# Both key halves of the probability-value products in one unit of TensorE's order

## The chip, the cores and the metric

The kernel runs on one core of a Trainium2 chip (trn2). The metric is the device time of one execution in microseconds. TensorE (PE) does the matrix products, ScalarE (ACT), VectorE (DVE) and GpSimd (POOL) the rest; SyncE (SP) issues the DMAs. Each engine works through its own instruction list in order, and they wait for each other on semaphores.

## The reference

The input is 32 batches of 256 tokens with 256 features. Four layers follow one another, each adding to x: an autocorrelation mix of a context, a mixture of 8 experts (router, top 1), an attention with 16 heads over 256 keys, and a gated feed-forward with quantised weights and activations. The part that matters here is the attention:

```
scores = jnp.einsum('bhqd,bhkd->bhqk', q, k) / jnp.sqrt(D_K)
scores = jnp.where(m == 0, NEG, scores)
p_attn = softmax(scores, axis=-1)
x = jnp.einsum('bhqk,bhkd->bhqd', p_attn, v)
```

## The kernel before

After a first stage over all batches (the context mix, up to about 160 us), the batches run through a software pipeline. One step of it starts one new batch and carries each older batch a stage on; some six batches are in work at once. A step is 128 ticks long. The table AT gives each job the tick at which it stands, counted from the batch's start, LATER shifts it on one engine, and CHUNKS says in how many pieces a job comes and how many ticks lie between them. The function pipeline sorts the pieces by tick within the step, for each engine by itself. A tick is only an order: the hardware knows the instruction list and the semaphores, nothing of ticks. The first eight steps and the rest are written out one after another.

The attention of a batch, for 16 heads and two halves of the keys (128 each):

- "max": PE multiplies queries and keys (L1312) into one of two banks, and DVE reduces to the maximum of each row (L1046). The negated maximum is written into an extra row of the query stack.
- "exp": for s = 0 to 15, PE computes the scores, keys on the partitions, of two heads and one key half (L1259) into cbank, which is one bank of PSUM. ACT takes the exponential (L796) into pt[s % 4], a ring of four buffers. Scores s wait for exponential s-1, since there is only one cbank. In s, bit 0 is the pair of heads, bit 1 the key half, and s // 4 the group of four heads.
- "pv": unit u = 0 to 7 (L1274) handles group u // 2 and key half u % 2. It is four matmuls with 32 columns of values each, into the four partition quarters of obank, which reads pt buffers 2u % 4 and 2u % 4 + 1. A matmul of fp32 data shows as two records in the profile, so a unit is eight records. Key half 0 starts the sum and key half 1 ends it. After each unit a semaphore pv_done[u % 2] is raised.
- "out": ACT copies obank to ot (L802), once per group.

The exponential s may overwrite its buffer once the unit that read it is done. With u = s // 2 - 2 it waits for pv_done of unit u, for s = 0 to 3 of the previous batch (units 6 and 7). On PE, unit u stands at tick 499 + 16u, group g's second unit thus at 515 + 32g; on ACT exponential s stands at 486 + 8s and "out" g at 524 + 32g.

On PE, what stands around the units within one step, in order (numbers are pieces; the jobs belong to batches of different age):

```
... v, score 0, xT_a, q, unit 7, route, score 1, h_T 1, norm 0, score 2, norm 1, unit 0,
routeT, down 1, score 3, norm_T, k, gateT, o, gbias, score 4, expert 0, unit 1, max 0,
score 5, max 1, expert 1, max 2, score 6, max 3, expert 2, unit 2, max 4, quant_T, score 7,
... score 8, max 7, gate_up 1, expert 4, unit 3, max 8, score 9, ... expert 6, unit 4, max 12,
... gate_up 5, unit 5, score 13, gate_up 6, h_T 0, max_T, score 14, gate_up 7, unit 6, down 0 ...
```

On ACT, the list reads at the places of interest: h_quant 1, exp 0, xah (xT_a, L747), q (L781), out 3, exp 1; gbias, exp 4, k (L770), out 0, exp 5; gate_up 0, exp 8, expert 3, gate_up 1, out 1, exp 9; h_quant 0, exp 12, expert 7, gate_up 5, out 2, exp 13, hqt (h_T 0, L853), max_T, gate_up 6, exp 14. Other engines' lists hold no pv job.

Of the kernel before, what the change touches and what calls it, by code (L numbers as in the profile page):

```python
# [15 lines left out]
NB, S, D = 32, 256, 256  # L16
# [32 lines left out]
    "load": 0, "x2": 211, "ln_a": 190, "xn_a": 228, "xT_a": 237, "route": 232, "routeT": 226, "gate": 233,  # L49
    "gateT": 257, "gbias": 267, "expert": 266, "k": 266, "k_split": 324, "k_write": 336, "ln_b": 311,  # L50
    "xn_b": 336, "xT_b": 350, "k_read": 440, "q": 363, "q_split": 380, "v": 354, "q_write": 366,
    "q_read": 449, "max": 393, "max_T": 449, "max_row": 619, "exp": 480, "pv": 499, "out": 511, "norm": 619,
    "norm_T": 645, "o": 666, "ln_c": 650, "absmax": 649, "quant": 646, "quant_T": 658, "gate_up": 672,
    "h_max": 710, "h_quant": 703, "h_T": 711, "down": 727, "store": 675,
}
# [24 lines left out]
    },  # L80
}

CHUNKS = {"expert": (8, 8), "max": (16, 4), "exp": (16, 8), "pv": (8, 16), "out": (4, 32), "norm": (2, 8),
          "gate_up": (8, 8), "h_max": (2, 32), "h_quant": (2, 32), "h_T": (2, 32), "down": (2, 32)}

BANKS = {
# [49 lines left out]
def after(eng, sem, b):  # L136

    if b.exists:
        eng.wait_ge(sem, b.n + 1)


def after4(eng, sem, b, k):

    if b.exists:
        eng.wait_ge(sem, b.fours(k))
# [19 lines left out]
def pipeline(eng, name, work):  # L165
# [3 lines left out]
    for order, (job, at) in enumerate(AT.items()):  # L169
        n, apart_by = CHUNKS.get(job, (1, 0))  # L170
        for c in range(n):
# [14 lines left out]
def build(nc, x, ctxT, mask, wq0, bq0, wout_r, bout, rwT, rb, ewT, eb, wqT, bq, wkT, bk, wvT, bv,  # L186
          woT, bo, wgT, wuT, wdT, out):
    with ExitStack() as ctx:
        def sb(name, shape, dt=F32):
            return ctx.enter_context(nc.sbuf_tensor(name, shape, dt))  # L190

        def sem(name):
            return ctx.enter_context(nc.semaphore(name))

        def sems(name, n):
            return [sem(f"{name}{i}") for i in range(n)]
# [67 lines left out]
        va = sb("va", [P, 2, T, H * 32])  # L264
        pt = sb("pt", [P, 4, 2, S])
# [86 lines left out]
        ebank, cbank, obank, maxb = bank[0:2], bank[3], bank[4], bank[7]  # L352
# [47 lines left out]
        sc_ready, ex_made, pv_done, ot_made = sems("sc_ready", 4), sems("ex_made", 4), sems("pv_done", 2), sem("ot_made")  # L400
# [722 lines left out]
        def _(pe):  # L1123
# [41 lines left out]
            for t in range(T):  # L1165
                for g in range(NG):
                    ins = pe.matmul(bank[t][:, 0:S], k0t[:, g, t * P:(t + 1) * P], q0t[:, g], start=(g == 0), stop=(g == NG - 1))
            ins.then_inc(lagstep, 1)

            for t, v in enumerate((bank[4], maxb)):  # L1170
                for g in range(NG):
                    ins = pe.transpose(v[:, g * P:(g + 1) * P], k0t[:, g, t * P:(t + 1) * P], ident[:])
# [5 lines left out]
            for t in range(T):  # L1178
                ins = pe.matmul(bank[2][0:1, 0:S], ones[:, 0:1], lagged[:, t], start=(t == 0), stop=(t == T - 1))
# [3 lines left out]
            for t in range(T):  # L1183
                for k in range(T):
                    ins = pe.matmul(bank[t][:, 0:D], circ[:, k, t * P:(t + 1) * P], wout_s[:, k], start=(k == 0), stop=(k == T - 1))
# [3 lines left out]
            for g in range(NG):  # L1189
                for k in range(T):  # L1190
                    ins = pe.matmul(bank[g // 2][:, (g % 2) * D:(g % 2) * D + D], v0[:, k, g * P:(g + 1) * P], wmix[:, k],
                                    start=(k == 0), stop=(k == T - 1))
# [22 lines left out]
            def work(job, c, b):  # L1215
                shared = shared_bank(job, c)
                par = b.par
                if job == "norm":
# [4 lines left out]
                    for g in range(4):  # L1223
                        ins = pe.transpose(shared[:, g * P:(g + 1) * P], ot[:, g, t * P:(t + 1) * P], ident[:])
                    ins.then_inc(otT_ready[t], 1)
                if job == "norm_T":
                    after(pe, on_made[1], b)
                    use(job, c, b, otn_made)
                    for k in range(KT):
                        for t in range(T):  # L1230
                            ins = pe.transpose(shared[:, k * S + t * P:k * S + (t + 1) * P], on[:, t, k * P:(k + 1) * P], ident[:])
                    ins.then_inc(onT_ready, 1)
                if job == "o":
                    after(pe, otn_made, b)
                    use(job, c, b, o_out)
                    for t in range(T):
                        for k in range(KT):
                            ins = pe.matmul(shared[:, t * D:(t + 1) * D], otn[:, k, t * P:(t + 1) * P], wo[:, k], start=(k == 0), stop=(k == KT - 1))  # L1238
                    ins.then_inc(op_ready, 1)
                if job == "quant_T":  # L1240
# [3 lines left out]
                    for k in range(KT):  # L1244
                        for t in range(T):
                            ins = pe.transpose(v[:, k * S + t * P:k * S + (t + 1) * P], xq[:, t, k * P:(k + 1) * P], identb[:])
                    ins.then_inc(xqT_ready, 1)
                if job == "exp":

                    s = c  # L1250
                    u, key = s // 2, (s // 2) % 2
# [5 lines left out]
                    for j in range(2):  # L1257
                        h = 4 * (u // 2) + 2 * (s % 2) + j
                        ins = pe.matmul(cbank[:, j * S:(j + 1) * S], ks[par][0:AROWS, h, key * P:(key + 1) * P],  # L1259
                                        qs[par][0:AROWS, h, :], start=True, stop=True)  # L1260
                    ins.then_inc(sc_ready[s % 4], 1)
                if job == "pv":

                    u = c
                    g, key = u // 2, u % 2
                    for i in (2 * u, 2 * u + 1):
                        after4(pe, ex_made[i % 4], b, i // 4 + 1)
                    if u == 0:
                        after(pe, va_made, b)
                        after4(pe, ot_made, b.ago(1), 4)  # L1270
                    elif key == 0:
                        after4(pe, ot_made, b, g)
                    for i in range(4):
                        ins = pe.matmul(obank[32 * i:32 * i + 32, 0:S],  # L1274
                                        va[:, par, key, (4 * g + i) * 32:(4 * g + i) * 32 + 32],
                                        pt[:, (2 * u + i // 2) % 4, i % 2], start=(key == 0), stop=(key == 1))
                    ins.then_inc(pv_done[u % 2], 1)
                if job == "gate_up":
                    t, n = c // 4, c % 4
                    if c == 0:  # L1280
# [2 lines left out]
                    for i, w in enumerate((wg, wu)):  # L1283
                        for k in range(KT):
                            ins = pe.matmul(shared[:, i * 256:(i + 1) * 256], xqt[:, k, t * P:(t + 1) * P],  # L1285
                                            w[:, k, n * 256:(n + 1) * 256], start=(k == 0), stop=(k == KT - 1))
                    ins.then_inc(gu_ready[c % 2], 1)
                if job == "h_T":
# [4 lines left out]
                    for k in range(IC):  # L1293
                        ins = pe.transpose(v[:, k * P:(k + 1) * P], hq[:, k * P:(k + 1) * P], identb[:])  # L1294
                    ins.then_inc(hqT_ready[t], 1)
                if job == "down":
# [3 lines left out]
                    for k in range(IC):  # L1300
                        ins = pe.matmul(shared[:, 0:D], hqt[:, k], wd[:, k], start=(k == 0), stop=(k == IC - 1))  # L1301
                    ins.then_inc(dn_ready[t], 1)
                if job == "max":
# [6 lines left out]
                    for j in range(2):  # L1310
                        h = 2 * p + j
                        ins = pe.matmul(shared[:, j * S:(j + 1) * S], qs[par][0:QROWS, h, t * P:(t + 1) * P],  # L1312
                                        ks[par][0:QROWS, h, :], start=True, stop=True)
                    ins.then_inc(mx_ready[t], 1)
                if job == "max_T":
# [3 lines left out]
                    for t in range(T):  # L1319
                        ins = pe.transpose(shared[0:H, t * P:(t + 1) * P], mx[:, t, :], ident[:])  # L1320
                    ins.then_inc(mxT_ready, 1)
                if job == "xT_b":
                    after(pe, xnb_made, b)
                    use(job, c, b, xbt_made)
                    for k in range(KT):
                        for t in range(T):
                            ins = pe.transpose(shared[:, k * S + t * P:k * S + (t + 1) * P], xn[:, t, k * P:(k + 1) * P], ident[:])
                    ins.then_inc(xnb_T, 1)
                if job == "q":
                    after(pe, xbt_made, b)  # L1330
                    use(job, c, b, qh_made)
                    for m in range(KT):
                        for k in range(KT):
                            ins = pe.matmul(shared[:, m * S:(m + 1) * S], wq[:, k, m * P:(m + 1) * P], xbt[:, k], start=(k == 0), stop=(k == KT - 1))
                    ins.then_inc(qp_ready, 1)
                if job == "v":
                    use(job, c, b, va_made)
                    for t in range(T):
                        for k in range(KT):
                            ins = pe.matmul(shared[:, t * D:(t + 1) * D], ct[:, par, k, t * P:(t + 1) * P], wv[:, k], start=(k == 0), stop=(k == KT - 1))  # L1340
                    ins.then_inc(vp_ready, 1)
                if job == "xT_a":
                    after(pe, xna_made, b)
                    use(job, c, b, xal_made)
                    for k in range(KT):
                        for t in range(T):
                            ins = pe.transpose(shared[:, k * S + t * P:k * S + (t + 1) * P], xn[:, t, k * P:(k + 1) * P], ident[:])
                    ins.then_inc(xna_T, 1)
                if job == "route":
# [3 lines left out]
                    for i, (w, v, k) in enumerate(ops):  # L1353
                        ins = pe.matmul(shared[:, 0:S], w[:, k], v[:, k], start=(i == 0), stop=(i == len(ops) - 1))
                    ins.then_inc(rt_ready, 1)
                if job == "routeT":
# [3 lines left out]
                    for t in range(T):  # L1360
                        ins = pe.transpose(shared[:, t * NE:(t + 1) * NE], lt[:, t * P:(t + 1) * P], ident[0:NE, 0:NE])
                    ins.then_inc(rtt_ready, 1)
                if job == "gateT":
                    after4(pe, rchain2, b, 4)
                    use(job, c, b, gt_made)
                    for t in range(T):
                        ins = pe.transpose(shared[0:NE, t * P:(t + 1) * P], gg[:, t], ident[:])
                    ins.then_inc(gT_ready, 1)
                if job == "gbias":
                    after(pe, gt_made, b)  # L1370
                    use(job, c, b, gb_out)
                    for t in range(T):
                        ins = pe.matmul(shared[:, t * D:(t + 1) * D], gt[:, t * P:(t + 1) * P], eb_s[:], start=True, stop=True)  # L1373
                    ins.then_inc(gb_ready, 1)
                if job == "k":
                    landed(pe, c_ld, b, 16)
                    use(job, c, b, kf_made)
                    for m in range(KT):
                        for k in range(KT):
                            ins = pe.matmul(shared[:, m * S:(m + 1) * S], wk[:, k, m * P:(m + 1) * P], ct[:, par, k], start=(k == 0), stop=(k == KT - 1))  # L1380
                    ins.then_inc(kp_ready, 1)
                if job == "expert":
# [7 lines left out]
                    for i, (v, w, k) in enumerate(ops):  # L1390
                        ins = pe.matmul(ebank[t][:, :], v[:, k, t * P:(t + 1) * P], w[:, k, p * 512:(p + 1) * 512],  # L1391
                                        start=(i == 0), stop=(i == len(ops) - 1))
                    ins.then_inc(e_ready[t], 1)

            pipeline(pe, "pe", work)


# [41 lines left out]
```

## Time and profile before

| | |
|---|---|
| median of 3 runs | 1781.84 us (1781.82 to 1786.88) |
| the profiled execution's own time | 1780.0 us |
| its span, first to last instruction | 1778.2 us |
| PE busy | 1570.2 us (88%) |
| DVE, ACT, POOL busy | 1198.3, 1097.4, 771.5 us |
| mean granted PE clock | 0.956 of full |
| chain that ended last, by engine | PE 51%, issue 16%, DVE 16%, POOL 6%, ACT 5%, DMA 5% |

The busy time of an engine is the sum over its instructions with overlaps taken once. The chain is followed back from the last instruction: at each step to what released it, or to the instruction before it on its engine.

### The profile page before, as it was taken

The page shows a single profiled execution, that of the slowest core. Times are in us where ns is not written, and L with a number is a line of the kernel's source. Part 1 is how long each engine was busy: PE and PEld are TensorE (multiplying, and loading weights), DVE is VectorE, ACT ScalarE, POOL GpSimd, SP SyncE. Part 2 cuts the span into 40 slices and gives each one's busy share as a digit, 9 for nine tenths or more (in the row PEclk, how much of TensorE's full clock was granted, in tenths as well). Part 3 has the DMA queues.
Part 4 walks back from the last instruction along what each step waited for, and adds up shares of the span by engine and source line. Part 5 has one row for each costly group of instructions (what it writes and reads, how often), then busy time and mean ns, then how long its engine had stood idle before and what let it go on. Part 6 is the DMA issues. An engine that isn't in the chain of part 4 may idle for free.

```text
span 1778.2 us, 33096 instructions
## 1 busy us (share of the span) xinstructions
PE 1570.2 (88%) x10422; PEld 1160.1 (65%) x10422; DVE 1198.3 (67%) x3300; ACT 1097.4 (62%) x2422; POOL 771.5 (43%) x962
## 2 busy tenths in 40 slices
PE   5935789999999999999999999999999999999764
PEld 4824556776666767666767776666676766676542
DVE  4882456777777777777777777777777777777533
ACT  1211246677776777776666666777776777666553
POOL 2374334444444444444444444444444444444211
PEclk9966899999999999999999999999999999999876
DMA  8722222233333232222222333333323322221100
GB/s 267 228 62 66 74 79 79 80 85 86 85 85 86 73 86 79 74 76 73 73 71 79 86 85 86 85 85 86 85 73 86 85 69 79 70 76 56 50 7 12
DMA packets 103169, 146.95 MB, mean 83 GB/s; under 512 B 11218, under 2 KB 98908, under 8 KB 99676
## 3 DMA queue, kind: packets, MB, share of 16 engines
q1 hardware_dynamic: 103004, 144.92, 29.3%
q8 instruction: 83, 1.36, 0.3%
q14 instruction: 82, 0.67, 0.1%
HBM read 99.79 MB, written 42.99 MB: 80 GB/s over the span
## 4 chain that ended last, share of the span: by engine, by line
PE 51%; issue 16%; DVE 16%; POOL 6%; ACT 5%; DMA 5%; SPq 1%; ACTq 0%; POOLq 0%; DVEq 0%
PE bank L1391 15%; PE bank L1312 7%; PE bank L1285 5%; PE bank L1259 5%; PE bank L1274 4%; DVE hm L1094 4%; PE bank L1238 2%; PE bank L1380 2%; DMA qs<-qsplit_d 2%; POOL hid L644 2%; PE bank L1294 2%; DMA qsplit_d<-pl 2%; PE bank L1373 1%; POOL rs L619 1%; PE bank L1301 1%
## 5 line engine op out<-in xcount | busy, mean ns | idle before, releaser
L796 ACT ACTIVATE pt<-bank 128x512 f32<-128x512 f32 x512 | 302.5, 591 | 204.4 <-PE bank L1259 204.3
L1046 DVE TENSOR_REDUCE mx<-bank 128x2 f32<-128x512 f32 x512 | 333.1, 682 | 45.2 <-PE bank L1312 43.0
L639 POOL TENSOR_TENSOR x<-x,et 128x256 f32<-128x256 f32 x256 | 190.1, 743 | 262.6 <-ACT et L830 262.5
L644 POOL TENSOR_TENSOR hid<-hid,t 128x256 f32<-128x256 f32 x256 | 187.4, 732 | 164.9 <-DVE t L1088 162.6
L1312 PE MATMUL bank<-ks,qs 96*128 96x256 f32 x1024 | 225.7, 304 | 28.0 <-DVE mx L1046 16.6
L1259 PE MATMUL bank<-qs,ks 98*128 98x256 f32 x1024 | 233.8, 310 | 15.1 <-ACT pt L796 13.4
L1312 PEld LDWEIGHTS bank<-ks,qs 96*128 96x128 f32 x1024 | 166.9, 191 | 101.9 <-DVE mx L1046 37.0
L1259 PEld LDWEIGHTS bank<-qs,ks 98*128 98x128 f32 x1024 | 159.3, 193 | 55.8 <-issue 25.8
L864 DVE BATCH_NORM_STATS2 bn<-x 128x6 f32<-128x256 f32 x256 | 95.8, 415 | 122.6 <-POOL x L648 92.3
L1391 PE MATMUL bank<-ewh,xah 128*128 128x512 f32 x512 | 174.7, 422 | 0.4 <-ACT et L830 0.2
L1088 DVE SCALAR_TENSOR_TENSOR t<-th,bank 128x256 f32<-128x256 f32 x256 | 106.9, 417 | 99.3 <-ACT th L842 90.6
L1274 PE MATMUL bank<-pt,va 128*32 128x256 f32 x2048 | 165.5, 395 | 0.8 <-ACT pt L796 0.8
L1391 PE MATMUL bank<-ewl,xah 128*128 128x512 f32 x512 | 161.0, 395 | 0.0
L1391 PE MATMUL bank<-ewh,xal 128*128 128x512 f32 x512 | 160.7, 395 | 0.0
L1016 DVE SCALAR_TENSOR_TENSOR x<-bank,gg,x 128x256 f32<-128x256 f32 x256 | 123.3, 481 | 47.2 <-PE bank L1391 35.7
L648 POOL TENSOR_TENSOR x<-x 128x512 f32<-128x512 f32 x32 | 40.9, 1277 | 253.9 <-ACT x L811 253.9
L830 ACT ACTIVATE et<-bank,gg 128x256 f32<-128x256 f32 x256 | 120.1, 469 | 26.1 <-DVE x L1016 22.7
L842 ACT ACTIVATE th<-bank,ts_ 128x256 f32<-128x256 f32 x256 | 122.8, 480 | 0.2 <-DVE t L1088 0.2
L847 ACT ACTIVATE hid<-hid,magic,hf 128x1024 f32<-128x1024 f32 x64 | 79.4, 1240 | 54.5 <-DVE hf L1101 54.5
L1391 PEld LDWEIGHTS bank<-ewl,xah 128*128 128x128 f32 x512 | 96.6, 189 | 23.5
L1391 PEld LDWEIGHTS bank<-ewh,xal 128*128 128x128 f32 x512 | 96.5, 189 | 22.9
L1285 PE MATMUL bank<-wg,xqt 128*128 128x256 bf16 x512 | 103.9, 286 | 4.4 <-DVE t L1088 3.5
(186 smaller groups left out, 3135.8 us busy)
## 6 DMA issues: line engine op xcount, KB each, us to landing
ks<-ksplit_d SPq DMA_DIRECT2D x96, 256.0 KB
qs<-qsplit_d SPq DMA_DIRECT2D x96, 256.0 KB, 4.2
x<-in_x SPq DMA_DIRECT2D x32, 256.0 KB, 3.0
va<-in_ctxT SPq DMA_DIRECT2D x32, 256.0 KB, 2.9
xl<-in_x SPq DMA_DIRECT2D x32, 256.0 KB
ct<-in_ctxT SPq DMA_DIRECT2D x32, 256.0 KB, 5.1
ksplit_d<-ph SPq DMA_DIRECT2D x32, 256.0 KB, 2.2
ksplit_d<-pl SPq DMA_DIRECT2D x32, 256.0 KB, 2.5
```

The costliest lines, as they stand in the source:

```text
L639: pool.tensor_tensor(x3[:, b.quad, t], x3[:, b.quad, t], et[:], ALU.add).then_inc(e_sum[t], 1)
L644: pool.tensor_tensor(part_, part_, t1[:], ALU.mult).then_inc(hid_made[c % 2], 1)
L796: act.activation(pt[:, s % 4].rearrange("p a c -> p (a c)"), cbank[:, :], ACT.Exp).then_inc(ex_made[s % 4], 1)
L830: act.activation(et[:], ebank[t][:, D:2 * D], ACT.Copy, scale=gg[:, t, 2 * p + 1:2 * p + 2])\
L842: act.activation(th[:], shared[:, 0:256], ACT.Tanh, scale=ts_[:, c // 4:c // 4 + 1])\
L1016: dve.scalar_tensor_tensor(out=x3[:, b.quad, t], in0=ebank[t][:, 0:D], scalar=gg[:, t, 2 * p:2 * p + 1], in1=x3[:, b.quad, t], op0=ALU.mul ...
L1046: dve.tensor_reduce(mx[:, t, 2 * p:2 * p + 2], shared[:].rearrange("p (h s) -> p h s", h=2), AX_X, ALU.max).then_inc(mx_made[t], 1)
L1259: ins = pe.matmul(cbank[:, j * S:(j + 1) * S], ks[par][0:AROWS, h, key * P:(key + 1) * P], qs[par][0:AROWS, h, :], start=True, stop=True)
L1274: ins = pe.matmul(obank[32 * i:32 * i + 32, 0:S], va[:, par, key, (4 * g + i) * 32:(4 * g + i) * 32 + 32], pt[:, (2 * u + i // 2) % 4, i % ...
L1285: ins = pe.matmul(shared[:, i * 256:(i + 1) * 256], xqt[:, k, t * P:(t + 1) * P], w[:, k, n * 256:(n + 1) * 256], start=(k == 0), stop=(k ...
L1312: ins = pe.matmul(shared[:, j * S:(j + 1) * S], qs[par][0:QROWS, h, t * P:(t + 1) * P], ks[par][0:QROWS, h, :], start=True, stop=True)
L1391: ins = pe.matmul(ebank[t][:, :], v[:, k, t * P:(t + 1) * P], w[:, k, p * 512:(p + 1) * 512], start=(i == 0), stop=(i == len(ops) - 1))
```

## The change

The eight pv units of a batch become four. Unit g holds both key halves of group g: it waits for the four exponentials of the group, does the four matmuls of key half 0, raises pv_done[0], does the four of key half 1, raises pv_done[1]. It stands on PE at tick 515 + 32g, where the second unit of the group stood; the places at 499 + 32g are empty. The number of matmuls, their shapes, the buffers and the waits of the other engines are as before.

```diff
-    ... "exp": 480, "pv": 499, "out": 511, ...
+    ... "exp": 480, "pv": 515, "out": 511, ...
-CHUNKS = {... "exp": (16, 8), "pv": (8, 16), "out": (4, 32), ...
+CHUNKS = {... "exp": (16, 8), "pv": (4, 32), "out": (4, 32), ...
                 if job == "pv":
-                    u = c
-                    g, key = u // 2, u % 2
-                    for i in (2 * u, 2 * u + 1):
-                        after4(pe, ex_made[i % 4], b, i // 4 + 1)
-                    if u == 0:
+                    g = c
+                    if g == 0:
                         after(pe, va_made, b)
                         after4(pe, ot_made, b.ago(1), 4)
-                    elif key == 0:
+                    else:
                         after4(pe, ot_made, b, g)
                     for i in range(4):
-                        ins = pe.matmul(obank[32 * i:32 * i + 32, 0:S],
-                                        va[:, par, key, (4 * g + i) * 32:(4 * g + i) * 32 + 32],
-                                        pt[:, (2 * u + i // 2) % 4, i % 2], start=(key == 0), stop=(key == 1))
-                    ins.then_inc(pv_done[u % 2], 1)
+                        after4(pe, ex_made[i], b, g + 1)
+                    for key in range(2):
+                        for i in range(4):
+                            ins = pe.matmul(obank[32 * i:32 * i + 32, 0:S],
+                                            va[:, par, key, (4 * g + i) * 32:(4 * g + i) * 32 + 32],
+                                            pt[:, 2 * key + i // 2, i % 2], start=(key == 0), stop=(key == 1))
+                        ins.then_inc(pv_done[key], 1)
```

## Rows read from the trace of the kernel before

**Rows 1.** Windows: stretch, length, busy PE, PEld, DVE, ACT, POOL, granted clock, DMA.
```profile
1000.00:1047.20 47.20, 44.94 (x314) 33.12 (x312) 34.22 (x95) 33.16 (x75) 21.84 (x29) 1.00 0.30 80
```

**Rows 2.** The chain of waits, 975 to 1005: start, length, what.
```profile
984.02 0.58 ACT pt L796
...
985.12 0.70 DVE xal L972
```

**Rows 3.** The page's costliest groups: busy, mean ns, idle before, what ended it.
```profile
L796 ACT ACTIVATE pt<-bank 128x512 f32<-128x512 f32 x512 | 302.5, 591 | 204.4 <-PE bank L1259 204.3
```

**Rows 4.** Timeline of PE, 1028 to 1046: start, length, instruction, idle before.
```profile
1029.50 0.48 PE L1259 MATMUL bank<-qs,ks 98*128 98x256 f32 x2 [0.18 <-ACT pt L796]
...
1030.26 1.89 PE L1334 MATMUL bank<-xbt,wq 128*128 128x256 f32 x8
1032.08 0.64 PE L1274 MATMUL bank<-pt,va 128*32 128x256 f32 x8
1033.07 0.51 PE L1354 MATMUL bank<-xah,rwh 128*128 128x256 f32 x2 [0.35 <-DVE xal L972]
...
1035.87 0.64 PE L1274 MATMUL bank<-pt,va 128*32 128x256 f32 x8
...
1036.66 1.05 PE L1301 MATMUL bank<-wd,hqt 128*128 128x256 bf16 x8
...
1044.31 0.63 PE L1391 MATMUL bank<-ewh,xal 128*128 128x512 f32 x2
1044.87 0.64 PE L1274 MATMUL bank<-pt,va 128*32 128x256 f32 x8
1045.44 0.51 PE L1312 MATMUL bank<-ks,qs 96*128 96x256 f32 x2
1045.78 0.40 PE L1259 MATMUL bank<-qs,ks 98*128 98x256 f32 x2
```

**Rows 5.** Timeline of ACT, 1028 to 1048.
```profile
1028.78 0.58 ACT L796 ACTIVATE pt<-bank 128x512 f32<-128x512 f32 x1
...
1031.23 0.58 ACT L796 ACTIVATE pt<-bank 128x512 f32<-128x512 f32 x1
1031.71 0.59 ACT L747 ACTIVATE xah<-bank 128x512 fp32r<-128x512 f32 x1
...
1035.10 1.00 ACT L853 ACTIVATE hqt<-bank 128x1024 bf16<-128x1024 bf16 x1
...
1043.64 0.60 ACT L796 ACTIVATE pt<-bank 128x512 f32<-128x512 f32 x1
...
1045.58 0.39 ACT L802 ACTIVATE ot<-bank 128x256 f32<-128x256 f32 x1 [0.82 <-PE bank L1274]
```

**Rows 6.** Timeline of DVE and of PE, 1049 to 1052.
```profile
1049.64 0.68 DVE L1046 TENSOR_REDUCE mx<-bank 128x2 f32<-128x512 f32 x1
...
1050.43 0.50 PE L1312 MATMUL bank<-ks,qs 96*128 96x256 f32 x2
```

**Rows 7.** Timeline of ACT and of PE, 1054 to 1057.
```profile
1054.59 0.60 ACT L796 ACTIVATE pt<-bank 128x512 f32<-128x512 f32 x1 [1.08 <-PE bank L1259]
...
1056.57 0.64 PE L1274 MATMUL bank<-pt,va 128*32 128x256 f32 x8
```

**Rows 8.** Timeline of all engines, 1067 to 1072.
```profile
1067.22 0.58 ACT L796 ACTIVATE pt<-bank 128x512 f32<-128x512 f32 x1
...
1067.71 0.64 PE L1274 MATMUL bank<-pt,va 128*32 128x256 f32 x8
...
1068.28 0.51 PE L1259 MATMUL bank<-qs,ks 98*128 98x256 f32 x2
...
1069.84 1.02 ACT L853 ACTIVATE hqt<-bank 128x1024 bf16<-128x1024 bf16 x1 [0.27 <-PE bank L1294]
...
1071.83 0.38 PE L1301 MATMUL bank<-wd,hqt 128*128 128x256 bf16 x2 [0.41 <-DVE narrow L1050]
```

**Rows 9.** Line L747 alone: ns min, median, max; first and last start.
```profile
L747 ACT ACTIVATE xah<-bank x32: 586/587/597, 160.2 to 1600.5; 128x512 fp32r<-128x512 f32 x32
```

More of the change, by code:

```diff
@@ L51 @@
     "xn_b": 336, "xT_b": 350, "k_read": 440, "q": 363, "q_split": 380, "v": 354, "q_write": 366,
-    "q_read": 449, "max": 393, "max_T": 449, "max_row": 619, "exp": 480, "pv": 499, "out": 511, "norm": 619,
+    "q_read": 449, "max": 393, "max_T": 449, "max_row": 619, "exp": 480, "pv": 515, "out": 511, "norm": 619,
     "norm_T": 645, "o": 666, "ln_c": 650, "absmax": 649, "quant": 646, "quant_T": 658, "gate_up": 672,
@@ L81 @@
 }
-CHUNKS = {"expert": (8, 8), "max": (16, 4), "exp": (16, 8), "pv": (8, 16), "out": (4, 32), "norm": (2, 8),
+CHUNKS = {"expert": (8, 8), "max": (16, 4), "exp": (16, 8), "pv": (4, 32), "out": (4, 32), "norm": (2, 8),
           "gate_up": (8, 8), "h_max": (2, 32), "h_quant": (2, 32), "h_T": (2, 32), "down": (2, 32)}
```

## The prediction

> **What bounds the kernel now.** I read the table of busy time, then the windows, then the chain of waits, then the timelines engine by engine. The window of one batch period [rows 1] shows TensorE (PE) busy 44.94 of 47.20 us at the full granted clock of 1.00, so the first idea is that every matmul removed is time won. The chain of waits corrects that: PE is on the chain for long stretches, but once a period it leaves PE and runs through ACT's exponential and, behind the copy of xah, DVE's xal [rows 2], back to PE's route product. In that place PE waits for ACT, and what moves ACT's exponential moves the whole step. The exponential itself waits a lot: 204.4 us idle before it, nearly all for score products [rows 3]. So the question is not what the probability-value (pv) products cost, but whom they release.
>
> Names: units 0 to 7 are the pv units of before; group g stands where unit 2g+1 stood and does the work of units 2g (half a, key half 0) and 2g+1 (half b). T is the time at which the unit at that place starts in the profiled step. "exp s" is ACT's s-th exponential of a batch, "score s" the product that feeds it. There is one score bank, so score s+1 waits for exp s; and there are four pt buffers, so exp s waits until the pv unit that read buffer s mod 4 is done. That last wait is what the change moves: exp 4, 8, 12 and exp 0 of the next batch waited for units 0, 2, 4 and 6, which stood 16 ticks before units 1, 3, 5, 7; now they wait for half a of groups 0, 1, 2, 3.
>
> **Prices.** A unit takes 0.57 us to the start of what follows (1044.87 to 1045.44) [rows 4]; the pair ahead of it lasts 0.56 to its start, where a record of full width takes 0.23 (eight in 1.82 us, 1030.26 to 1032.08), so 0.10 goes at the entry. A unit that disappears from a full PE gives 0.67. Half b, behind half a in the same shape, is not in this trace: two full-width records are 0.46, a whole unit is 0.57, I take 0.48. Half a ends at T+0.64 (the unit's length). From a PE end to ACT is 0.07 (1045.51 to 1045.58), from an ACT end to PE 0.14 (1029.36 to 1029.50) [rows 4, 5]. Two ACT operations start 0.48 apart (1031.23 to 1031.71).
>
> The number of matmuls is unchanged, no DMA is moved, and only PE's queue is reordered: ACT, DVE, POOL and SP keep their order. The edits of the AT and CHUNKS entries and of the loop are these moves and nothing else; the register and semaphore instructions saved I put at 0 (the ends are 0 and the 0.10 of the entry, already counted).
>
> **Group 3 (T = 1032.08).** Before, exp 0 of the next batch ran at 1031.23, since unit 6 was long done. Now it waits for half a: 1032.08 + 0.64 + 0.07 = 1032.79, 1.56 us later. Behind it in ACT's queue stands the copy of xah (1031.71, becomes 1033.27), for which DVE's xal waits, for which PE's route product waits (1033.07, already with 0.35 us idle for xal). All of them follow, the four copies of q and out 3 too. Half b is hidden in that wait: group 3 would end at 1033.13. PE can't start group 3 earlier: it stands behind the eight q products. Loss 1.56; ends 1.38 (half a counted as done two records of 0.23 after its start) and 1.60.
>
> **Unit 0 (1035.87) disappears.** PE is full here. What follows after the two small transposes is down (1036.66), which waits for ACT's hqt, ready at 1036.10 and seen by PE at 1036.24. So of 0.67 only 0.42 is won; ends 0.67 and 0.
>
> **Group 0 (T = 1044.87).** exp 4 ran at 1043.64 and now runs at T+0.71, ends T+1.31, and score 5 can start at T+1.45; before it started at T+0.91 (1045.78). PE's own work would have let it start at T+1.39, so the two are nearly level. Loss 0.54; ends 0.46 and 0.65. Behind exp 4 on ACT wait the copy of k, out 0 and exp 5; those feed POOL's split and PE's expert 2, which comes one whole expert product later: I put that at 0.
>
> **Unit 2 disappears.** What follows is max 4, at 1050.43 [rows 6]. Its bank is free only when DVE's reduction, which ran from 1049.64 for 0.68, ends at 1050.32. PE would have waited there anyway: gain 0 (ends 0 and 0.11).
>
> **Group 1 (T = 1056.57) and unit 4.** exp 8 goes from 1054.59 [rows 7] to 1057.28. The same sum as in group 0 gives +0.54, and unit 4 in the full PE stretch behind it gives back 0.67: -0.13. But the 2.69 us delay of ACT passes to DVE, whose gate product waits for ACT's tanh, and four reductions of 0.68 [rows 6] stand behind it. I estimate that DVE loses what is left and put the pair at 0; ends -0.13 and +0.20.
>
> **Group 2 (T = 1067.71).** exp 12 ran at 1067.22, now at T+0.71; it ends at T+1.29, and score 13 starts at T+1.43 instead of T+0.57 (1068.28): +0.86 [rows 8]. No max product stands between them, so nothing covers it. The transposes of h and ACT's copy hqt (1069.84) come 0.86 later, and with them the small copies, tanh and normalisations behind them on ACT, up to the exponentials with which group 3 begins. Loss 0.86; ends 0.50 (ACT's work catches up) and 1.00.
>
> **Unit 6 disappears** where PE then waits for DVE's "narrow" (0.41 us idle at 1071.83) [rows 8]: gain 0, ends 0 and 0.10.
>
> **Sum.** Group 3's loss needs an exp 0 with a batch before it and a route two batches ahead: batches 1 to 29, 29 times (the xah copies end at 1600.5 [rows 9], as the front stages do). 29 x 1.56 = 45.2. The rest, -0.42 + 0.54 + 0 + 0.86 = 0.98, counts for 30 batches (the last two run with the front stages gone): 29.4. Together 74.6 us on the profiled execution's own 1780.0 (span 1778.2): 1854.6. The median of the runs is 1.8 higher: 1856. With all ends low it is 29 x 1.38 + 30 x (-0.67 + 0.46 - 0.13 + 0.50 - 0.11 - 0.10) = 40.0 - 1.5 = 38.5, with all high 29 x 1.60 + 30 x (0 + 0.65 + 0.20 + 1.00) = 101.9; not all fall on one side, so the likeliest case's own range is 1834 to 1878.
>
> A rule of the Trainium skill speaks for the change. "TensorEngine Tiling (Array Packing)", section Key Properties, says that changing the tiling mode drains TensorE; the 0.10 at the entry above agrees with it. By that rule alone the sum would be the gain of rival B.
>
> **Rivals.**
> B, the other side: PE's busy time decides. Each of 4 x 32 = 128 merges turns a unit of 0.67 into a half of 0.48, 0.19 saved, 24 us in all: 1757. It decides if exp 4, 8, 12 and 0 have at least as much slack as they are delayed. For it: PE busy 95% of a period. Against it: PE's 0.35 us idle for xal, an ACT product, right behind group 3, and the 1.56 that ACT is moved.
> C, exp 0's delay is absorbed (the xah chain has slack that I don't see), the other losses stand: 30 x 0.98 = 29 us, 1811. Against it: the chain of waits names that very chain.
> D, no change: the gain of 0.67 each from units 2, 4 and 6 comes through after all and offsets C's losses; within 5 us of 1782.
> E, the delays add up: ACT's or DVE's lateness costs another 1 us or more a period, by longer PE waits or because PE, idle more, is granted less than 1.00; above 1886. For it: ACT work behind three of the moved exponentials. Against: ACT's spare time.
> The change does what it says: the order follows from the ticks, with nothing to fall back on.
>
> **How the numbers follow.** Forecast 0.70, C 0.11, B 0.08, E 0.08, D 0.03. 1856 us, range 1812 to 1880 (all of the likeliest case's but its top and the upper part of C's). Differences under 0.3% are what a measurement of this kernel can't tell from none. Faster: B, 0.08. Same: D, 0.03. Slower: 0.89.
>
> **What would show it.** After: the period 49.4 to 50.0 us instead of 47.2; exp 0 directly behind group 3's half a, and PE idle for xal some 1.4 us ahead of the route product; 16 records of pv in one piece; next product 1.05 us behind its start (0.57 + 0.48); score 13 idle about 0.4 us for exp 12; ACT idle more before the exponential with pv as releaser. A period shorter than 47.2 would prove the argument wrong at its root, one near 48.2 would say that exp 0's delay is hidden.

## The result, and the profile after

The changed kernel takes 1875.91 us (median of 4 runs, 1874.01 to 1876.36) against 1782.95 us of the kernel before on the same chips: a ratio of 1.0515, with a 95% interval of 1.0496 to 1.0534. It is slower by 93 us. Forecast were 1856 us, a range of 1812 to 1880, and 0.89 for slower.

The page of the profile after: the span, and the group of ACT's exponentials that answers to [rows 3]. Behind the second bar stands the idle time before them and what ended most of it.

```profile
span 1874.6 us, 33096 instructions
...
L796 ACT ACTIVATE pt<-bank 128x512 f32<-128x512 f32 x512 | 305.0, 596 | 362.4 <-PE bank L1274 266.0
...
L1274 PE MATMUL bank<-pt,va 128*32 128x256 f32 x2048 | 139.5, 391 | 0.8 <-ACT pt L796 0.8
```

The same 512 exponentials wait 362 us instead of 204, and the releaser is no longer the score product (L1259) but the pv product (L1274), 266 us of it. The pv products themselves fell to 139.5 us, from 165.5 on the page of before: the merge does make them cheaper, by 26 us, as rival B had it. The kernel lost 93 all the same. The waits of the whole execution say it in order (who waited for whom: us in total, times, longest):

```profile
ACT pt L796 <- PE bank L1274: 266.0, 125, 4.3
...
DVE xal L972 <- ACT xah L747: 82.7, 32, 8.7
...
PE bank L1354 <- DVE xal L972: 46.6, 30, 1.6
```

125 waits are four a batch, but for three: exp 0, 4, 8 and 12. The window of one period, which answers to [rows 1]:

```profile
1000.00:1050.31 50.31, 45.00 (x314) 33.77 (x313) 33.99 (x94) 33.02 (x75) 21.84 (x29) 1.00 0.25 70
```

From copy of xah to copy of xah a period is 50.31 us (the median over the steady part) where it was 47.23. In this steady part PE's busy time in a period is what it was, at the same full granted clock, and what was added is idle. The first two periods with attention in them are different. The windows of both kernels, from copy of xah to copy of xah, before first:

```profile
233.36:275.14 41.78, 35.95 (x218) 26.23 (x217) 21.24 (x56) 20.50 (x48) 13.91 (x17) 0.96 0.29 81
275.14:322.37 47.23, 45.10 (x303) 33.08 (x302) 33.73 (x93) 32.38 (x75) 21.88 (x28) 1.00 0.28 77
```
```profile
234.62:281.82 47.20, 41.45 (x232) 30.33 (x230) 21.13 (x56) 20.36 (x48) 13.97 (x17) 0.86 0.31 83
281.82:334.31 52.49, 47.20 (x296) 34.97 (x296) 33.67 (x93) 32.24 (x75) 21.84 (x28) 0.93 0.23 66
```

There the changed kernel ran at a lower mean clock, 0.86 and 0.93 where the kernel before had 0.96 and 1.00.

Group 3's place, a timeline of PE, ACT and DVE, answering to [rows 4, 5]:

```profile
581.96 0.47 PE L1259 MATMUL bank<-qs,ks 98*128 98x256 f32 x2 [0.42 <-ACT pt L796]
...
582.71 1.89 PE L1334 MATMUL bank<-xbt,wq 128*128 128x256 f32 x8
...
584.53 1.07 PE L1274 MATMUL bank<-pt,va 128*32 128x256 f32 x16
585.30 0.60 ACT L796 ACTIVATE pt<-bank 128x512 f32<-128x512 f32 x1 [1.65 <-PE bank L1274]
585.79 0.59 ACT L747 ACTIVATE xah<-bank 128x512 fp32r<-128x512 f32 x1
...
586.41 0.69 DVE L972 TENSOR_TENSOR xal<-bank,xah 128x512 fp32r<-128x512 f32 x1 [2.04 <-ACT xah L747]
...
587.16 0.50 PE L1354 MATMUL bank<-xah,rwh 128*128 128x256 f32 x2 [1.56 <-DVE xal L972]
```

PE starts the 16 records; 0.77 us later, when half a is done, ACT may start exp 0; xah follows 0.49 behind it, then xal, then the route product, for which PE stood idle for 1.56 us. From the start of the pv products to route it is 2.63 us; before it was 0.99. Groups 1 and 2, answering to [rows 7, 8]:

```profile
560.70 1.07 PE L1274 MATMUL bank<-pt,va 128*32 128x256 f32 x16
561.47 0.60 ACT L796 ACTIVATE pt<-bank 128x512 f32<-128x512 f32 x1 [3.83 <-PE bank L1274]
561.71 0.50 PE L1312 MATMUL bank<-ks,qs 96*128 96x256 f32 x2
...
562.12 0.50 PE L1259 MATMUL bank<-qs,ks 98*128 98x256 f32 x2
...
563.10 0.42 DVE L1088 SCALAR_TENSOR_TENSOR t<-th,bank 128x256 f32<-128x256 f32 x1 [3.18 <-ACT th L842]
```
```profile
572.09 1.07 PE L1274 MATMUL bank<-pt,va 128*32 128x256 f32 x16
...
572.86 0.60 ACT L796 ACTIVATE pt<-bank 128x512 f32<-128x512 f32 x1 [1.15 <-PE bank L1274]
...
573.51 0.50 PE L1259 MATMUL bank<-qs,ks 98*128 98x256 f32 x2 [0.34 <-ACT pt L796]
```

In group 1, ACT had been idle for 3.83 us ahead of exp 8, and DVE 3.18 us ahead of the gate product behind it: the exponential's wait holds up everything in ACT's queue. The next product follows at T+1.01, so half b costs 0.44 behind the 0.57 of a unit.

### The profile page after: what moved, and what is told of

It reads as the page before. It is cut to its first block, busy times and chain, and to the rows that moved or that the text cites. A ratio compares the mean times of both kernels' runs of the same rounds, so it can differ in the third digit from the quotient of the medians.

```text
span 1874.6 us, 33096 instructions
## 1 busy us (share of the span) xinstructions
PE 1577.8 (84%) x10422; PEld 1185.1 (63%) x10422; DVE 1189.4 (63%) x3300; ACT 1092.1 (58%) x2422; POOL 770.9 (41%) x962
## 4 chain that ended last, share of the span: by engine, by line
PE 52%; issue 16%; DVE 14%; ACT 9%; POOL 4%; DMA 4%; SPq 1%; ACTq 0%; POOLq 0%; DVEq 0%
PE bank L1391 14%; PE bank L1312 6%; PE bank L1259 5%; PE bank L1274 5%; PE bank L1285 4%; PE bank L1334 2%; PE bank L1380 2%; PE bank L1238 2%; DVE hm L1094 2%; DVE mx L1046 2%; DVE x L1016 2%; DMA qs<-qsplit_d 2%; PE bank L1373 2%; PE bank L1301 1%; ACT pt L796 1%
## 5 line engine op out<-in xcount | busy, mean ns | idle before, releaser
L1259 PE MATMUL bank<-qs,ks 98*128 98x256 f32 x1024 | 240.1, 316 | 38.2 <-ACT pt L796 32.4
L1259 PEld LDWEIGHTS bank<-qs,ks 98*128 98x128 f32 x1024 | 159.0, 193 | 96.0 <-ACT pt L796 53.6
L1274 PE MATMUL bank<-pt,va 128*32 128x256 f32 x2048 | 139.5, 391 | 0.8 <-ACT pt L796 0.8
L665 POOL TENSOR_TENSOR pl<-pf,ph 128x512 fp32r<-128x512 f32 x32 | 40.8, 1276 | 202.4 <-ACT ph L781 202.4
```

The source lines that it names most:

```text
L1274: ins = pe.matmul(obank[32 * i:32 * i + 32, 0:S], va[:, par, key, (4 * g + i) * 32:(4 * g + i) * 32 + 32], pt[:, 2 * key + i // 2, i % 2], ...
```

## The experiments

Theory A: the loss is the later start of exp 4, 8, 12 and 0, each with its own consequences. Rival R: the long piece of 16 records costs by itself, wherever it stands. Ratios are to the kernel before on the same chip, with 95% intervals. The versions that treat groups apart list their units in two small tables, which the first diff shows once.

**Group 3 split again.**

```diff
-CHUNKS = {... "pv": (4, 32), ...
+CHUNKS = {... "pv": (5, 0), ...
+PV_TICKS = [515, 547, 579, 595, 611]
+PV_PARTS = [(0, (0, 1)), (1, (0, 1)), (2, (0, 1)), (3, (0,)), (3, (1,))]
 ...
-            age, tick = divmod(at + LATER[name].get(job, 0) + c * apart_by, TICKS)
+            at_c = PV_TICKS[c] if job == "pv" else at + c * apart_by
+            age, tick = divmod(at_c + LATER[name].get(job, 0), TICKS)
 ...
-                    g = c
+                    g, keys = PV_PARTS[c]
 ...
-                    for key in range(2):
+                    for key in keys:
```

The lines marked by points that are left out make each piece wait only for the exponentials of its own key halves, as the units of before did.

> As the changed kernel, but group 3's work stands again as two units, 6 and 7, at their two old places; groups 0 to 2 stay merged. Theory A (the moved waits of ACT's exponentials cost): exp 0 runs before group 3 again, the 1.60 us a period that the two traces differ by at this place go away, 29 times: 46 us off 1876, about 1830 (1822 to 1838). Rival R (the long piece of 16 records itself costs, wherever it stands): one merge in four is undone, a quarter of the 93 us: about 1853.

Measured 1820.11 us, 1.0218 (1.0201 to 1.0235); the period is 48.53. More came back than A said (56 of the 93 us, not 46, so the time lies below A's range), and far more than a quarter: R fails. Group 3 costs 1.78 us a period on top of the others. The trace of this kernel shows why that is more than the forecast 1.56 (L851 quantises h, L800 is exp 0, L751 the copy of xah, L1280 unit 7):

```profile
669.00 1.24 ACT L851 ACTIVATE hid<-hid,magic,hf 128x1024 f32<-128x1024 f32 x1 [0.60 <-DVE hf L1105]
...
670.15 0.57 ACT L800 ACTIVATE pt<-bank 128x512 f32<-128x512 f32 x1
...
670.63 0.58 ACT L751 ACTIVATE xah<-bank 128x512 fp32r<-128x512 f32 x1
...
671.12 0.64 PE L1280 MATMUL bank<-pt,va 128*32 128x256 f32 x8
```

Here exp 0 follows ACT's own queue and starts 0.97 us ahead of unit 7; in the kernel before it was 0.85 (1031.23 and 1032.08). With groups 0 to 2 merged, PE's q products have fallen 0.12 us further behind than ACT. A merged group 3 makes exp 0 wait for PE until 0.77 behind its start, so it costs 0.85 + 0.77 = 1.62 us in the kernel before and 0.97 + 0.77 = 1.74 of the 1.78 here.

**The waits alone.** No matmul moves; exponentials wait for the second unit of a group instead of the first.

```diff
-                    u = s // 2 - 2
+                    u = (s // 2 - 2) | 1
                     if u >= 0:
-                        after4(act, pv_done[u % 2], b, u // 2 + 1)
+                        after4(act, pv_done[1], b, u // 2 + 1)
                     else:
-                        after4(act, pv_done[u % 2], b.ago(1), (u + 8) // 2 + 1)
+                        after4(act, pv_done[1], b.ago(1), (u + 8) // 2 + 1)
```

> The kernel before, with its eight units and their places, but every exponential that waited for the first unit of a group now waits for the second unit of that group. No matmul moves and none is merged. A: exp 4, 8, 12 and 0 come as late as in the changed kernel: +0.54, +0.54 and about 0.25 behind it, +0.86, +1.56 a period, with nothing given back by the units 0 and 4 that stay: 3.75 us x 30 = 112, about 1895 (1875 to 1905). R: no merged piece, so no loss: 1783.

Measured 1900.64 us, 1.0671 (1.0652 to 1.0689), period 51.19, 3.96 more than before. That is the whole loss and more, with eight units in their old places and shapes. The merge is not the cause of the loss; it takes a part of it back.

**All four merged, but earlier.** One line: "pv" at 510 instead of 515.

> As the changed kernel, all four groups merged, but the merged unit stands at tick 510 + 32g instead of 515 + 32g: directly behind score 4g+4, ahead of expert 0, gate_up 1 and expert 4, max 15, and for group 3 ahead of xT_a and q. A: the exponentials are delayed by 0.7 us less the 0.25 that they waited for the score anyway, and exp 0 not at all; group 3 pushes q back by about 1 us instead, which ACT's copies of q pass on. Some 0.2 us a period is saved at groups 0 to 2 and some 0.6 lost at group 3: 1775 to 1805. R: four merged pieces as before, so 1876.

Measured 1802.30 us, 1.0115 (1.0098 to 1.0132), period 47.92. Four merged pieces cost 20 us here and 93 five ticks further on. As expected by A, inside its range.

**Groups 0 to 2 merged and early, group 3 split.** PV_TICKS = [510, 542, 574, 595, 611].

> Groups 0 to 2 merged and standing directly behind score 4, 8 and 12 (ticks 510, 542, 574), group 3 as the two units 6 and 7 at their old places. A: no exponential is late by more than about 0.45 us, exp 0 not at all, and three changes of the array's shape a period are saved at 0.19 each: 0.3 to 0.6 us a period under before, 1765 to 1775. R: three merged pieces, so three quarters of 93 us: about 1853.

Measured 1781.46 us, 0.9993 (0.9978 to 1.0008): no difference. R fails again, but my 10 us and more of gain did not come either. Laid over the period of before, event by event from the copy of xah, the trace has PE 0.27 early where unit 0 is missing, 0.15 late after group 0, 0.59 late after group 1, 0.18 early where unit 4 is missing, and DVE's reduction over hid at the same time to within 0.03. The merged pieces stand ahead of expert 0 and gate_up 1 now and push them back; what PE then regains ends at a reduction that DVE starts no earlier.

**One group at a time.** PV_PARTS with a single merged group at its changed place, all other units as before.

> Only group 0 is merged (at its changed place), groups 1 to 3 stand as two units each at their old places. A (each merge costs what its own moved exponential delays, less what its removed unit gives back): the two traces show -0.26 at unit 0 and +0.62 at group 0, 0.36 us a period, 30 times: 1793 (1789 to 1796). Rival R2 (the merges spend one shared slack, and a single one is mostly absorbed): under 1787.

> Only group 1 is merged; unit 4 stays where it was. A: nothing is won at unit 2, and by the end of the stretch behind it the traces are 0.85 us further apart, which in the changed kernel the missing unit 4 then gave back (0.75). Here it gives nothing back: 0.85 x 30 = 25, 1807 (1800 to 1812). R2: under 1790.

> Only group 2 is merged. A: the gain at unit 4 (0.7 on PE) is lost at DVE's reduction over hid, which does not start earlier, so what is left is exp 12: 0.85 a period, 30 times, 1808 (1800 to 1811). R2: under 1790.

> Only group 3 is merged. A: exp 0 of the next batch and the copy of xah behind it come 1.6 us late and nothing takes it back: 1.6 x 29 = 46, 1829 (1822 to 1838; the difference between the changed kernel and its version with group 3 split was 56, so it may be the upper part). R2: under 1806, since group 3's loss would need the others'.

| merged | us | ratio (95%) | period, against 47.23 |
|---|---|---|---|
| group 0 | 1791.81 | 1.0052 (1.0038 to 1.0066) | 47.59, +0.36 |
| group 1 | 1806.37 | 1.0145 (1.0114 to 1.0176) | 48.05, +0.82 |
| group 2 | 1782.78 | 1.0003 (0.9990 to 1.0017) | 47.30, +0.07 |
| group 3 | 1829.25 | 1.0265 (1.0238 to 1.0291) | 48.86, +1.63 |
| sum of the four | | | +2.88 |
| all four | 1875.91 | 1.0515 (1.0496 to 1.0534) | 50.31, +3.08 |

Three came out as A said, and the four periods add up to nearly all of the change: the losses are nearly each their own, and no shared slack of R2's size is there. Group 2 came out below A's range by 17 us (by 25 from its point), where R2 had it, but for another reason. The kernel with only group 2 merged, DVE, PE and ACT (the line numbers are 4 to 6 higher: L800 is the exponential, L1280 pv, L1263 the score, L1098 the reduction over hid):

```profile
546.84 1.21 DVE L1098 TENSOR_REDUCE hm<-hid 128x1 f32<-128x1024 f32 x1
...
549.47 0.50 PE L1318 MATMUL bank<-ks,qs 96*128 96x256 f32 x2 [0.63 <-DVE mx L1050]
...
550.36 1.07 PE L1280 MATMUL bank<-pt,va 128*32 128x256 f32 x16
551.12 0.60 ACT L800 ACTIVATE pt<-bank 128x512 f32<-128x512 f32 x1 [1.15 <-PE bank L1280]
551.77 0.50 PE L1263 MATMUL bank<-qs,ks 98*128 98x256 f32 x2 [0.34 <-ACT pt L800]
```

The loss at exp 12 is there as forecast: score 13 at T+1.41, PE idle for 0.34. But from the copy of xah (514.99) to the reduction it is 31.85 us, and in the period of before 32.45: with unit 4 gone from the full stretch, everything comes 0.60 earlier, DVE's reduction too. I had read the opposite out of the kernel before this table, where the delay of groups 0 and 1 had eaten that lead. So unit 4 gives 0.6 and exp 12 takes it away.

**Group 2 alone, earlier.** If that is so, the 0.60 can be kept by having half a done before ACT wants exp 12. PV_TICKS = [499, 515, 531, 547, 574, 595, 611], then 572.

> Only group 2 is merged, and it stands directly behind score 12 (tick 574) instead of at 579; all other units as before. A: with the merge at 579 the trace had DVE's reduction over hid 0.60 us earlier (unit 4 gone) and lost it again at exp 12 (+1.25). At 574 half a ends before ACT is ready for exp 12, so most of the 0.60 stays: 0.4 to 0.6 us a period, 12 to 18 us off before: 1764 to 1770. If the lead is absorbed behind it by DVE's or POOL's queue: 1782.

> As the one with group 2 alone at 574, but ahead of max 14 and score 12 (tick 572). A: the same lead of 0.60, exp 12 itself 0.3 us later than with 574 since its score is; 1765 to 1774. If absorbed: 1782.

Measured 1761.11 us, 0.9870 (0.9854 to 0.9887), and 1761.04 us, 0.9878 (0.9861 to 0.9894); both periods 46.59. Faster than before, by 0.64 us a period; both times lie below their forecast ranges, by 3 and 4 us, and standing ahead of score 12 cost nothing.

**Unit 4 moved, nothing merged.** PV_TICKS = [499, 515, 531, 547, 574, 579, 595, 611], every unit with one key half.

> The kernel before with eight units, nothing merged: only unit 4 moves, from tick 563 to 574, directly behind score 12, where PE waits for DVE ahead of max 15. If the gain of the kernel with group 2 merged at 574 comes from the place (unit 4 out of the full stretch into an idle one), this gives the same: a period of 46.6 us, 1761 (1758 to 1765). If it comes from the merge (fewer changes of the array's shape), nearly all of it goes: 1776 to 1783.

Measured 1760.19 us, 0.9890 (0.9871 to 0.9910), period 46.59. The same gain with no merge at all, so it is the place. First the hole in the kernel before, then this run:

```profile
1066.82 0.50 PE L1312 MATMUL bank<-ks,qs 96*128 96x256 f32 x2 [0.47 <-DVE mx L1046]
```

```profile
538.73 1.21 DVE L1098 TENSOR_REDUCE hm<-hid 128x1 f32<-128x1024 f32 x1
...
540.32 0.40 PE L1263 MATMUL bank<-qs,ks 98*128 98x256 f32 x2
...
540.62 0.68 DVE L1050 TENSOR_REDUCE mx<-bank 128x2 f32<-128x512 f32 x1
...
540.66 0.64 PE L1280 MATMUL bank<-pt,va 128*32 128x256 f32 x8
...
541.35 0.50 PE L1318 MATMUL bank<-ks,qs 96*128 96x256 f32 x2
...
541.76 0.57 ACT L800 ACTIVATE pt<-bank 128x512 f32<-128x512 f32 x1
```

Unit 4 fills the hole ahead of max 15 (L1318), in which PE had waited for DVE (0.47 us in the period of before), and max 15 starts 0.05 behind the reduction that it needs, which ends at 541.30. Exp 12 waits for nobody.

**One wait alone, exp 0 and 1.** The kernel before, with only these two waiting for unit 7 instead of unit 6.

```diff
                     else:
-                        after4(act, pv_done[u % 2], b.ago(1), (u + 8) // 2 + 1)
+                        after4(act, pv_done[1], b.ago(1), (u + 8) // 2 + 1)
```

> The kernel before, eight units at their places, with one wait moved: exp 0 and exp 1 wait for unit 7 of the previous batch instead of unit 6. A: this alone is group 3's loss, since unit 7 ends where half a of group 3 ended: 1.6 us a period x 29, 1828 (1824 to 1834), as with group 3 alone merged. R (the piece of 16 records costs): 1782.

Measured 1856.81 us, 1.0413 (1.0394 to 1.0432): R fails, but the loss is 73 us, not 47. Of its 27 steady periods 14 last 50.4 us or a little more, most of the others (8 of 13) 48.9, as with group 3 alone merged, and none of them over 49.9. In each of the 14, and in no other, the granted clock falls behind the wait. Windows of six us from the copy of xah on, one of a long period and two of others, columns as in [rows 1]:

```profile
576.20:582.20 6.00, 4.64 (x34) 3.98 (x34) 2.58 (x8) 4.79 (x11) 1.27 (x1) 0.72 0.46 156
626.60:632.60 6.00, 4.66 (x46) 3.92 (x47) 3.62 (x16) 4.53 (x11) 1.27 (x1) 1.00 0.49 159
725.60:731.60 6.00, 4.57 (x46) 3.83 (x46) 3.63 (x15) 4.62 (x11) 1.27 (x1) 1.00 0.46 157
```
```profile
574.93 0.64 PE L1274 MATMUL bank<-pt,va 128*32 128x256 f32 x8
577.56 0.50 PE L1354 MATMUL bank<-xah,rwh 128*128 128x256 f32 x2 [1.99 <-DVE xal L972]
...
578.61 1.04 PE L1294 MATMUL bank<-identb,hq 128*128 128x128 bf16 x8
```

At a mean of 0.72 the 6 us hold 34 products instead of 46: for part of them PE runs at the lower of its two levels, 1.2 GHz, and the eight transposes of h last 1.04 us instead of 0.62. The event-by-event comparison of one such period gives 1.53 us for it. 14 such falls are 21 us, and 73 - 21 = 52 is the exponential's own loss, near the 48 of group 3 alone. Before each fall PE had stood idle for 1.99 us; but it did so in every period, and 13 kept the clock, as did all steady periods of the kernel with the waits alone, where PE is idle for 1.99 us as well. Its window of 1300 us, with a clock of 1.00:

```profile
350.00:1650.00 1300.00, 1162.92 (x7922) 845.00 (x7921) 868.31 (x2381) 836.96 (x1877) 555.36 (x712) 1.00 0.27 73
```

In the changed kernel half b fills 0.43 of that idle time, 1.56 is left, and none of its 27 steady periods lost the clock; the period before them, with the same 1.56, did (0.93, the window of 281.82 above).

## Why the prediction was right

The direction, the mechanism and the largest term were right; the time was 20 us short, 4 us inside the upper end of the range. That it stayed inside owes something to the width of the range, since part of what was missing (the lower clock of the first periods) stood in no term of the sum. The period, forecast at 49.4 to 50.0 us, is 50.31.

- Group 3, the wait of exp 0: forecast 1.56 us a period, measured 1.61 in the comparison of the two traces, 1.63 alone, 1.78 as the last of four, for the reason given with its split. Its chain (exp 0, xah, xal, route) is the one that the timeline shows, and PE's idle time before route is 1.56 where 1.4 was expected.
- Unit 0: forecast -0.42, the traces show -0.26. The prediction had only down wait for ACT's hqt, and the two small transposes of lt run in that wait. They wait for it too (the rows are below the list).
- Group 0: forecast +0.54, the traces show +0.62. Score 5 starts at T+1.41, 0.50 later; the pair that follows its wait adds 0.1, a pair at the full rate having become a slow one. Sum with unit 0: +0.36, the same as alone.
- Unit 2: forecast 0, measured 0 (0.03 at most). Max 4 comes where DVE lets it.
- Group 1 with unit 4: forecast 0, ends -0.13 and +0.20, traces +0.25. This is the largest error. Exp 8 passes its 2.7 us to tanh, the gate product and DVE's reductions, which made group 1 cost 0.85 by the traces, 0.82 alone, where the sum for PE gave 0.54. The missing unit 4 gave PE back 0.75, more than the 0.67 of the prices, and 0.15 of that was lost again ahead of max 15.
- Group 2: forecast 0.86, the traces show 0.85, with score 13 at T+1.42. But as a price of merging group 2 it was wrong: unit 4's lead belongs to it, and the two cancel.
- The count: 29 or 30 periods at one price. The first two with attention in them grew by 5.4 and 5.3 us, from 41.8 to 47.2 and from 47.2 to 52.5, 4.5 more than two normal ones. These are the periods with the lower granted clock in the windows above; by the mean clocks some 8.6 us of full-speed TensorE time are missing there against the kernel before (an estimate from the four windows), of which 4.5 would be what came through. With only group 0 merged the first of them also shows 0.85 and grew by 2.6 us, where a steady period grew by 0.36; with only group 3 merged it shows 0.96 and the two grew by no more than two normal ones. Together with 3.08 instead of 2.54 a period, some 15 us over 28 periods, that accounts for the 18 us between 74.6 and 93.
- Prices: half b 0.44, forecast 0.48; next product at T+1.01, forecast T+1.05; half a releases ACT at T+0.77, forecast T+0.71. A unit that disappears from a full PE gives 0.78 (unit 4, in the kernel with only unit 4 moved), forecast 0.67: the pair behind a unit takes 0.34 to what follows it (1045.44 to 1045.78), where one in a full-width stretch takes 0.24, and this 0.10 was left out.

The rows for unit 0, from the changed kernel:

```profile
589.16 1.00 ACT L853 ACTIVATE hqt<-bank 128x1024 bf16<-128x1024 bf16 x1
...
590.26 0.26 PE L1361 MATMUL bank<-ident,lt 8*128 8x8 f32 x2 [0.26 <-issue]
...
590.45 1.05 PE L1301 MATMUL bank<-wd,hqt 128*128 128x256 bf16 x8
```

PE is idle for 0.26 us ahead of the transposes of lt, not of down. By the kernel's table BANKS they write the bank that hqt is copied from, and they start 0.10 behind that copy's end (590.16); down follows 0.19 later. The profile names no releaser here: the bank is read from the code, and the times fit it.

Rival B's saving exists: 0.78 - 0.44 = 0.34 a merge where nothing waits, and the kernel with the waits alone is 25 us slower than the one with waits and merges. As a gain over the kernel before it came through in no run here: the rule of the Trainium skill ("TensorEngine Tiling (Array Packing)", Key Properties: changing the tiling mode drains TensorE) bears on PE's time only, and the place of a unit decides whose time it is. In the end, one unit in a better place gave 21 us, and merging added nothing to it (both periods 46.59). Rival D is out; C is out, since nothing absorbed exp 0's delay. Rival E's lower clock came in the first two periods with attention and in no steady one; in the kernel with one wait moved, where PE idled 0.43 us longer, it came in 14 of 27 steady ones.

Open: what makes the clock of the first periods lower when group 0 is merged, and by what the idle time of 1.99 us sometimes costs the clock and sometimes doesn't.

## What to carry to other kernels

When work is put together, look at the first half's consumers: the release moves to the place of the merged piece, and every instruction queued behind the waiting one moves with it. Price each place by itself, by who is late there: the same matmuls cost 0.78 us in a full stretch of PE, nothing in front of a wait, and 1.6 when an exponential hangs on them. Before merging, try moving: the idle times of the bound engine are free slots.

## What the runs showed of the hardware

- A piece of 16 records of 32 columns costs 1.01 us to the next product, one of 8 costs 0.57, and each costs 0.10 more at the entry and 0.10 in the pair behind it. Eight records more in the same piece cost 0.44, a piece of their own 0.77 to 0.78: some 0.33 for going into and out of the shape once.
- A semaphore raised within a running piece of matmuls reaches ACT 0.77 us after the piece's start, where 0.64 to its records' end and 0.07 were expected.
- An idle time of 1.99 us of PE, once a period, cost the full clock in 14 of 27 periods of one kernel, 1.53 us each, and in none of another with the same idle time; with 1.56 us, in the changed kernel and in the one with group 3 alone merged, in no steady period.
